# Layer norms' roots as one power on GpSimd, a padded router held while tokens stream, dispatch as steps of its own

## The reference

```python
# attn: 16 heads of 16
h = ln(x); xc = silu(causal_conv4(h))
q, k = l2norm(h@Wq), l2norm(h@Wk); v = ln_per_head(h@Wv)
i = sigmoid(xc@Wig + big); gamma = sigmoid(xc@Wg + bg)
mem_t = gamma_t * mem_{t-1} + (i*k*v)_t
o = groupnorm(ln_per_head(mem) * q) * sigmoid(xc@Wog + bog)
h = x + o@Wo; h2 = ln(h)
out = h + (silu(h2@Wgate) * (h2@Wval)) @ Wout          # hidden width 1024
# moe: 8 experts of 176, top 2 by softmax(x@router.T), weights normalised
routed = sum over the 2 experts of w_e * (silu(x@gate_e) * (x@up_e)) @ down_e
shared = sigmoid(x@shared_gate_w) * (silu(x@sw_gate)*(x@sw_up)) @ sw_down   # width 704
```

## Time and profile before

| | us |
|---|---|
| median of 3 runs | 605.73 |
| lowest, highest | 604.96, 609.38 |
| the profiled execution | 608.32 |
| its span, first to last instruction | 605.9 |
| PE, DVE, ACT, POOL busy | 526.0, 394.4, 261.8, 112.4 |

### The profile page before, as it was taken

How to read it: one execution, slowest core, us unless ns; L and a number is a source line. 1 busy time by engine, 2 the same in 40 slices (tenths; PEclk the granted TensorE clock), 3 DMA queues, 4 the chain that set the end, 5 groups by cost and what they waited for, 6 DMA issues and landing times.

```text
span 605.9 us, 8087 instructions
## 1 busy us (share of the span) xinstructions
PE 526.0 (87%) x2464; PEld 416.9 (69%) x2464; DVE 394.4 (65%) x1159; ACT 261.8 (43%) x465; POOL 112.4 (19%) x133
## 2 busy tenths in 40 slices
PE   2835358999669999999999998999998999999981
PEld 1413234678555687886678786888886799999871
DVE  6786644788774798876488792332649566766437
ACT  4721444625365424365621525311243556666404
POOL 1510003200002323002205000031006024444400
PEclk9985679999769999999999999799998989999997
DMA  8981000000010002111001010010007224444274
GB/s 277 417 235 36 2 2 0 2 10 26 35 35 1 0 19 88 36 35 36 0 2 71 0 36 35 1 41 30 35 8 262 63 64 131 117 140 123 70 273 138
DMA packets 29548, 44.41 MB, mean 73 GB/s; under 512 B 3211, under 2 KB 24203, under 8 KB 29163
## 3 DMA queue, kind: packets, MB, share of 16 engines
q1 hardware_dynamic: 24515, 32.95, 16.9%
q0 software_dynamic: 3408, 9.38, 4.1%
q10 hardware_dynamic: 1584, 1.57, 0.9%
HBM read 27.55 MB, written 16.34 MB: 72 GB/s over the span
## 4 chain that ended last, share of the span: by engine, by line
PE 74%; DVE 16%; ACT 5%; DMA 3%; issue 2%; POOL 0%; ACTq 0%; POOLq 0%; DVEq 0%; SPq 0%
PE psum L768 15%; PE psum L727 12%; PE psum L728 12%; PE psum L729 12%; PE psum L794 5%; PE psum L843 3%; PE psum L737 3%; PE psum L815 3%; DVE XC L1223 2%; PE psum L811 2%; PE psum L829 2%; PE psum L918 1%; PE psum L935 1%; DMA QKV<-x 1%; PE psum L965 1%
## 5 line engine op out<-in xcount | busy, mean ns | idle before, releaser
L637 ACT ACTIVATE SM<-psum 128x512 f32<-128x512 f32 (+1 forms) x56 | 33.3, 596 | 135.0 <-PE psum L729 93.4
L1348 DVE TENSOR_TENSOR SM<-SM,psum 128x512 f32<-128x512 f32 (+1 forms) x56 | 38.3, 683 | 52.4 <-ACT SM L637 48.1
L513 POOL DMA_INDIRECT x_dispatched<-XN,dest x32 | 35.5, 1109 | 163.2 <-DVE XN L1416 154.6
L768 PE MATMUL psum<-WOU,SM 128*128 128x256 f32 x256 | 59.8, 379 | 0.0
L794 PE MATMUL psum<-WQKV,HT 128*128 128x512 f32 (+1 forms) x128 | 51.4, 554 | 6.3 <-ACT QKV L572 2.7
L504 POOL TENSOR_TENSOR OG<-QKV,hvec 128x256 f32<-128x256 f32 x16 | 13.4, 835 | 230.2 <-ACT IG L579 213.4
L768 PEld LDWEIGHTS psum<-WOU,SM 128*128 128x128 f32 x256 | 48.3, 189 | 10.1 <-issue 2.9
L522 POOL DMA_INDIRECT y_routed<-GO,g_dest x39 | 37.7, 967 | 64.1 <-ACT GO L702 63.4
L794 PEld LDWEIGHTS psum<-WQKV,HT 128*128 128x128 f32 x128 | 26.4, 214 | 29.7 <-issue 23.5
L768 PE MATMUL psum<-SDN,SM 128*128 128x256 f32 (+1 forms) x192 | 44.6, 381 | 0.0
L768 PEld LDWEIGHTS psum<-SDN,SM 128*128 128x128 f32 (+1 forms) x192 | 35.8, 189 | 6.6 <-issue 1.3
(11 more groups left out here) (292 smaller groups left out, 1321.2 us busy)
## 6 DMA issues: line engine op xcount, KB each, us to landing
XG<-x_dispatched SPq DMA_DIRECT2D x39, 130.0 KB, 2.7
YF<-y_routed SPq DMA_DIRECT2D x4, 1024.0 KB, 9.1
RUPR<-rup SPq DMA_DIRECT2D x1, 2816.0 KB
X<-x SPq DMA_DIRECT2D x4, 512.0 KB, 6.4
x_after_attention<-X SPq DMA_DIRECT2D x4, 512.0 KB, 2.8
QKV<-x ACTq DMA_DIRECT2D x3, 512.0 KB
y_shared<-SH SPq DMA_DIRECT2D x3, 512.0 KB, 2.9
SHF<-y_shared SPq DMA_DIRECT2D x1, 1536.0 KB
```

What stands on the lines that cost most here:

```text
L513: nc.gpsimd.indirect_dma_start(XD[:, :], bass.IndirectOffsetOnAxis(dest[:, i, old + j:old + j + 1], 0), XN[:, j, :], None).then_inc(dispat ...
L637: nc.scalar.activation(SM[0:rows, g % 3, 0:tb], p_pair(n)[0][0:rows, 0:tb], ACT.Silu).then_inc(silu_ready, 1)
L768: last = nc.tensor.matmul(p_down[:, j // 2, (j % 2) * D:(j % 2 + 1) * D], SM[0:rows, g % 3, j * P:(j + 1) * P], weight[0:rows, m, :], star ...
L1348: nc.vector.tensor_tensor(SM[0:rows, g % 3, 0:tb], SM[0:rows, g % 3, 0:tb], value_rows(n, rows)[:, 0:tb], ALU.mult).then_inc(hid_ready, 1)
```

## The change

**Roots.** The eighteen `rsqrt` calls of layer norms over 256 values (`ln0`, `ln2`, `sum`, `x2`, each once per block, and the two final groups) go. DVE signals `var_ready`, POOL raises variance plus epsilon to the power -0.5 in one `tensor_tensor` with a tile of -0.5 as second operand, signals `root_ready`, and DVE waits for that before the shift. For `ln0` the wait stands at step 2, two steps behind the statistics; for `ln2` and `x2` at step 1, with the shift; for `sum` at step 2; for the final groups at once behind the statistics. The per-head roots stay.

**Router.** Its 9 columns are padded to 128 with zeros and are now the weights of the array; 512 tokens stream: 2 halves x 3 products. The result has the logits on 9 partitions. ACT copies it to LGT, which lies in the memory of SH and so waits for the previous block's store of SH. A new step `logit` turns it back, four PE transposes of 9x128, and DVE copies to LG.

**Choice and dispatch.** `choose` 3 (the weights and tags, DVE) now stands before `rank` (PE and DVE), and the eight indirect DMAs are four steps `send` of two, in blocks 0 to 2 one behind each of the next hidden tiles' down products.

**Memory and loads.** The raw router weights, wg16, wmean and wgx now lie under RUPR and RDNR. So SP waits for `wr_lo` and `wg_ready` before it loads RUPR, and it loads RDNR only behind the last block's stores of `x_after_attention` and `y_shared`, with a wait for the last block's `mup`.

The core of the diff:

```diff
-RP = RW + 1
+RP = P
...
-        late = {0: [("choose", b - 1, 1)], 1: [("choose", b - 1, 2)], 2: [("rank", b - 1, 0), ("choose", b - 1, 3)]} if b > 0 else {}
+        late = {0: [("choose", b - 1, 1)], 1: [("choose", b - 1, 2)], 2: [("choose", b - 1, 3), ("rank", b - 1, 0)],
+                **{m: [("send", b - 1, m - 3)] for m in range(3, 3 + TILES[b - 1])}} if b > 0 else {}
...
-            order += [("xt", b, 0), ("route", b, 0), ("choose", b, 0)]
-    route = {4: [("xt", b, 0)], 5: [("route", b, 0), ("choose", b, 0)], 6: [("choose", b, 1)], 7: [("choose", b, 2)],
-             8: [("rank", b, 0), ("choose", b, 3)]}
+            order += [("xt", b, 0), ("route", b, 0), ("logit", b, 0), ("choose", b, 0)]
+    route = {4: [("xt", b, 0)], 5: [("route", b, 0)], 6: [("logit", b, 0), ("choose", b, 0), ("choose", b, 1)], 7: [("choose", b, 2)],
+             8: [("choose", b, 3), ("rank", b, 0)] + [("send", b, j) for j in range(TILES[b])]}
...
+            wr, wg16, wmean, _, wgx = (first_names.enter_context(nc.sbuf_tensor(k, s, F32)) for k, s in (
+                ("wr", [P, C, RP]), ("wg16", [P, C, HEADS]), ("wmean", [P, C, HEADS]),
+                ("under_rupr", [P, E * C * GU - C * (RP + 2 * HEADS)]), ("wgx", [P, C, D])))
...
+        minus_half = sb("minus_half", [P, 2, max(FIN)])
...
+        LGT = SH[:, :, :].rearrange("p j d -> p (j d)")[0:RW, 0:TB]
...
+            sp.wait_ge(wr_lo, 1)
+            sp.wait_ge(wg_ready, 1)
             sp.dma_start(RUPR[:, :, :, :], rup).then_inc(w_in["routed"], 16)
-            sp.dma_start(RDNR[:, :, :, :], rdn).then_inc(w_in["routed"], 16)
...
             sp.wait_ge(up_psum, done("mup", NB - 1, FM - 1))
+            sp.dma_start(RDNR[:, :, :, :], rdn).then_inc(w_in["routed"], 16)
...
+            def root(kind, n, out, variance, power):
+
+                pool.wait_ge(var_ready[kind], n + 1)
+                nc.gpsimd.tensor_tensor(out, variance, power, ALU.pow).then_inc(root_ready[kind], 1)
+
+            link(nc.gpsimd.memset(minus_half[:, :, :], -0.5))
...
-                if (stage, m) == ("choose", 3):
-                    pool.wait_ge(xn_ready, new)
-                    pool.wait_ge(tag_ready, b + 1)
-                    pool.wait_ge(dest_ready, b + 1)
-                    for j in range(nj):
-                        for i in range(2):
-                            nc.gpsimd.indirect_dma_start(XD[:, :], bass.IndirectOffsetOnAxis(dest[:, i, old + j:old + j + 1], 0),
-                                                         XN[:, j, :], None).then_inc(dispatched, 16)
+                if stage == "send":
+                    if m == 0:
+                        pool.wait_ge(xn_ready, new)
+                        pool.wait_ge(tag_ready, b + 1)
+                        pool.wait_ge(dest_ready, b + 1)
+                    for i in range(2):
+                        nc.gpsimd.indirect_dma_start(XD[:, :], bass.IndirectOffsetOnAxis(dest[:, i, old + m:old + m + 1], 0),
+                                                     XN[:, m, :], None).then_inc(dispatched, 16)
+                if (stage, m) == ("ln0", 1):
+                    root("ln0", b, r01[:, b % 2, :, 0:nj], hva[:, :, 0:nj], minus_half[:, :, 0:nj])
...
+            for g in range(len(FIN)):
+                root("fin", g, fin_r[:, g % 2, 0:FIN[g]], va[:, 0:FIN[g]], minus_half[:, 0, 0:FIN[g]])
...
+                if stage == "route":
+                    act.wait_ge(rt_psum, b + 1)
+                    if b > 0:
+                        act.wait_ge(sh_kept, 16 * b if b < NB - 1 else 16 * (b - 1))
+                    nc.scalar.activation(LGT[:, 0:tb], p_token(b)[0:RW, 0, 0:tb], ACT.Copy).then_inc(rt_kept, 1)
...
+                    for c in range(C):
+                        last = mm3(p_token(b)[:, 0, 0:tb], wrH[:, c, :], wrL[:, c, :], part_h[:, c, 0:tb], part_l[:, c, 0:tb],
+                                   c == 0, c == C - 1)
+                    last.then_inc(rt_psum, 1)
+                if stage == "logit":
+                    pe.wait_ge(rt_kept, b + 1)
                     for j in range(nj):
-                        t = slice(j * P, (j + 1) * P)
-                        for c in range(C):
-                            last = mm3(p_token(b)[:, 0, j * RP:(j + 1) * RP], part_h[:, c, t], part_l[:, c, t], wrH[:, c, :], wrL[:, c, :],
-                                       c == 0, c == C - 1)
-                    last.then_inc(rt_psum, 1)
+                        last = nc.tensor.transpose(p_token(b)[:, 1, j * RW:(j + 1) * RW], LGT[:, j * P:(j + 1) * P], ident[0:RW, 0:RW])
+                    last.then_inc(rt_turned, 1)
...
-                    own = tuple(t[:, :, 0:nj] for t in (hva, hrs, hrt))
                     if m == 0:
                         dve.wait_ge(h_in, 16 * (b + 1))
-                        stats(nj, lambda j: QKV[:, j, 0:D], (hst, hmv, hva[:, 0, :]))
-                        step(nc.vector.tensor_scalar(hva[:, 1, 0:nj], hmv[:, 0:nj, 1], 1.0 + EPS, EPS * EPS, ALU.mult, ALU.add))
-                    if m == 1:
-                        settle()
-                        step(rsqrt(r01[:, b % 2, :, 0:nj], *own))
+                        link(stats(nj, lambda j: QKV[:, j, 0:D], (hst, hmv, hva[:, 0, :])))
+                        nc.vector.tensor_scalar(hva[:, 1, 0:nj], hmv[:, 0:nj, 1], 1.0 + EPS, EPS * EPS, ALU.mult,
+                                                ALU.add).then_inc(var_ready["ln0"], 1)
                     if m == 2:
-                        settle()
+                        dve.wait_ge(root_ready["ln0"], b + 1)
...
-                    link(rsqrt(l2r[:, 0:nj], *scratch(nj)))
+                    dve.wait_ge(root_ready["ln2"], b + 1)
                     minus_mean(nj, l2n, l2r, mv).then_inc(ln2_stats, 1)
...
-                if (stage, m) == ("sum", 1):
-                    step(rsqrt(ers[:, 0:nj], eva[:, 0:nj], ers[:, 0:nj], ert[:, 0:nj]))
+                    stats(nj, lambda j: HR[:, j, :], EXPERTS_OWN).then_inc(var_ready["sum"], 1)
                 if (stage, m) == ("sum", 2):
-                    settle()
+                    dve.wait_ge(root_ready["sum"], b + 1)
...
-                if stage == "route":
-                    dve.wait_ge(rt_psum, b + 1)
-                    nc.vector.tensor_copy(LG[:, 0:nj, :], p_token(b)[:, 0, 0:nj * RP].rearrange("p (j r) -> p j r", r=RP)[:, :, 0:RW]).then_inc(rt_copied, 1)
+                if stage == "logit":
+                    dve.wait_ge(rt_turned, b + 1)
+                    nc.vector.tensor_copy(LG[:, 0:nj, :], p_token(b)[:, 1, 0:nj * RW].rearrange("p (j r) -> p j r", r=RW)).then_inc(rt_copied, 1)
...
+                    dve.wait_ge(picked, b + 1)
...
-                aggregate(nj, (fst, fmv, va))
-                link(rsqrt(r[:, 0:nj], *scratch(nj)))
+                aggregate(nj, (fst, fmv, va)).then_inc(var_ready["fin"], 1)
+                dve.wait_ge(root_ready["fin"], g + 1)
```

More of the change, by code:

```diff
@@ L154, in steps @@
 def steps(engine):
-    attention = [(PLACE[engine][b][i] if b >= 0 else 0, s[0], b + (s in AHEAD), s[1]) for b in range(-1, NB)
+    attention = [(PLACE[engine][b + 1][i], s[0], b + (s in AHEAD), s[1]) for b in range(-1, NB)
                  for i, s in enumerate(ATTENTION) if 0 <= b + (s in AHEAD) < NB]
@@ L234, in build @@
         hst, hmv = sb("hst", [P, J, 6]), sb("hmv", [P, J, 2])
-        hva, hrs, hrt = (sb(k, [P, 2, J]) for k in ("hva", "hrs", "hrt"))
+        hva = sb("hva", [P, 2, J])
         vec = sb("vec", [P, C, NVEC])
         hvec = sb("hvec", [P, 4, HD])
-        wr, wrH, wrL = sb("wr", [P, C, RP]), sb("wrH", [P, C, RP], F32R), sb("wrL", [P, C, RP], F32R)
-        wg16, wgx = sb("wg16", [P, C, HEADS]), sb("wgx", [P, C, D])
-        wmean = sb("wmean", [P, C, HEADS])
+        wrH, wrL = sb("wrH", [P, C, RP], F32R), sb("wrL", [P, C, RP], F32R)
         st, mv = sb("st", [P, J, 6]), sb("mv", [P, J, 2])
         est, emv = sb("est", [P, J, 6]), sb("emv", [P, J, 2])
-        eva, ers, ert = (sb(k, [P, J]) for k in ("eva", "ers", "ert"))
+        eva, ers = (sb(k, [P, J]) for k in ("eva", "ers"))
+        minus_half = sb("minus_half", [P, 2, max(FIN)])
         va, rs, rt = (sb(k, [P, J * 2 * HEADS]) for k in ("va", "rs", "rt"))
@@ L291, in build @@
         ident_zero, ident_ready, halo_zero, same_head = map(sem, ("ident_zero", "ident_ready", "halo_zero", "same_head"))
+        var_ready, root_ready = ({k: sem(f"{k}_{what}") for k in ("ln0", "ln2", "sum", "x2", "fin")} for what in ("var", "root"))
         s_dve, s_act, s_pool = sem("s_dve"), sem("s_act"), sem("s_pool")
@@ L506, in at @@
                     nc.gpsimd.tensor_tensor(vj, vj, per_dim(1, 0), ALU.mult).then_inc(v_scaled, 1)
-                if (stage, m) == ("choose", 3):
-                    pool.wait_ge(xn_ready, new)
-                    pool.wait_ge(tag_ready, b + 1)
-                    pool.wait_ge(dest_ready, b + 1)
-                    for j in range(nj):
-                        for i in range(2):
```

(18 more changed lines are left out.)

8 lines of the change are left out of this document (4 added, 4 removed), and 58 rows, old and new, of the table PLACE.

## The result

The changed kernel takes 604.76 us (median of 13 runs, 602.02 to 607.84) beside 605.73 us of the kernel before (13 runs in turn with them): ratio 0.995, 95% interval 0.9928 to 0.9972. It is half a per cent faster, 3 us by the ratio; I had forecast 13.6. The profiled execution took 606.2 us (span 604.5) against 608.3 (span 605.9).

The account below looks back on a forecast made before the run. PE, busy 526.0 of 605.9 us, was taken as the bound, with DVE or POOL work counting in four places. Terms 7.3 + 1.0 + 1.0 + 1.0 + 1.0 + 0.5 + 1.8 = 13.6 us off 605.7 gave 592, range 586 to 604.

Parts of the forecast that it names:

- roots 4.5: Five exposed roots (block 0's first norm, `ln2` of blocks 0 and 1, both final groups) each 0.9 us shorter on POOL.
- wide router with its clock 5.8: Fewer, wider router products: 1.0 us each in blocks 1, 2 and 3, clock kept 1.0, the rest inside the hand-over.
- order 3.3: New step order: hand-over gain beyond roots and router, plus 0.5 us from weighing ahead of rank in block 3.
- load 0: RDNR loaded behind the last y_shared store, near ACT's use in the last block: cost 0, up to 3 us for the range.
- R: Round trip of a power from DVE over POOL and back: 0.7 us, between 0.3 and 1.8.
- Hand-over, 7.3: Block 0 to block 1, at 150 to 186 us: first hidden product at 178.1 instead of 185.4, 7.3 us saved.
- The opening: Block 0's attention, a serial chain: two exposed roots there save 1.8 us.
- End: Two exposed roots of the final groups: 1.8 us saved.
- third rival: New order gives back its savings (block 1's norm later, or half clock through the hand-over): 599, or 601 with RDNR late; chance 0.22.
- first rival: The power on POOL is slow: gain 9.6 us at R = 1.5, used up at 3.1; chance 0.09.

Follow-up runs that it names:

- the doubled powers: Changed kernel with each power computed twice on GpSimd: 612.68 us, 1.0096 of the kernel before.
- XN first: Changed kernel, RDNR loaded near 340 us, ACT's XN instructions ahead of the HT copies at the hand-over: 600.56 us, 0.9889; second set 600.91, 0.9905.
- the run with the router undone: Changed kernel with the 24 narrow router products back, without the copy and four transposes: 608.76 us, 1.0016 of the kernel before.
- early load: Changed kernel with RDNR's load issued after block 3's last gate product instead of behind its last hidden product: 602.32 us, 0.9929 of the kernel before.
- old order: Changed kernel's roots, router and loads in the kernel before's order of steps: 605.55 us, 0.9967; with RDNR loaded near 340 us 600.68, then 600.86.
- the second trace: Changed kernel run once more without any edit: 604.44 us, 0.9948 of the kernel before.
- both undone: Changed kernel with roots back on DVE and narrow router products, new order and loads kept: 619.63 us, 1.0192 of the kernel before.
- late load in the kernel before: Kernel before with RDNR's load moved from the opening to behind block 3's last hidden product: 611.16 us, 1.0055 of the kernel before.

## Why the prediction was wrong

It was wrong in size: the sign held, the gain was 3 us instead of 13.6. The sum falls into four parts: roots 4.5, wide router with its clock 5.8 (1.8 in the hand-over, four times 1.0), order 3.3 (the rest of the hand-over, and the rank), load 0. All four failed. Timed one by one, roots and router are 1.9 and 3.0 us, the order nothing that can be measured, and the load a loss of 3.3 in the kernel before.

1. **Roots, 4.5: mis-sized.** The count was right, as the doubled powers showed. R, the round trip of a power over POOL, was not: I took 0.7 between bounds of 0.3 and 1.8, and it is 1.12 at 128x4 and 1.74 at 128x8. My reason for the low end was size: a power of few elements is near the iota. But 128x4 to 128x8 adds 0.65 us, 0.16 us per element of a partition, some fifty times the product's 0.0033 (0.84 us for 256). Two narrow roots won 0.5 each, three wide ones lost 0.1 each: 0.7 us by the trace, 1.9 us [0, 3.8] timed. The first power of the run took 1.67 us, like the later ones of its size; the Trainium skill ("GPSIMD Engine Reference", section 2.1) has about 6 us for the first call of a freshly loaded kernel, and no run here shows such a cost.
2. **Hand-over, 7.3, measured 3.0.** The opening missed 1.7 (its two roots gave 0.1), and so OG's product came at 157.71, 1.3 later than my 156.4. `ln2` gave 0.5, not 0.9. Then I took HN to follow its statistics at once, as before. With the shorter DVE chain ACT became the chain: HT held XN up, XN held HN up, 1.2 us; and HN now stands ahead of XTH, so from HN to the router are 3.9 us where there were 2.5. The run with XN first gave 1.0 of this back. That the WO product waits for the HR add and statistics was priced right.
3. **Router, 5.8, measured alone 3.0 us [1.3, 4.5].** Block 1's 2.3 us beside 2.0 is the term that held, but its parts did not: 0.7 are the shorter work (5.2 to 4.5, by the run with the router undone, where 1.0 was forecast), and 1.6 the clock, where I had halved 1.9 for doubt. That the fall stood in the trace of the kernel before was luck: it is in three of six traces with narrow products. Block 2's products ran at half clock behind the same 2.01 us wait: 0.4, not 1.0. Block 3's own share is 0.6 (from its router to the next hidden product 8.89 us instead of 9.48), and a half clock from 447.4 us took it away again in this trace.
4. **Order, 3.3, measured about nothing.** Both new operations with the early load are 0.9879 and 0.9907 in the old order, 0.9889 and 0.9905 in the new one with XN first, 0.9929 [0.989, 0.9968] in the new one as it was. In the changed kernel's trace 1.2 us of what it gave at the hand-over went on ACT's queue there, and 1.0 in TensorE's wait before block 2's router.
5. **RDNR's load, 0, measured 3.3 in the kernel before: the cost that I had described and then put at nothing.** The text has the mechanism, "5 us late, in front of ACT's next silu", with its bound of 3. I took the lower end since RDNR stood behind one store only. It took 13.4 us from issue to use (448.25 to 461.67), more than sup's 10.9, with XF and SHF on its heels, and ACT wanted it at 455.4. In the changed kernel itself the load's cost is smaller and not clear of noise: 1.3 us by the ratios (0.9950 and 0.9929). From the first shared-expert product of the last block to the first waited-for expert product are 33.9 and 33.5 us in its two traces, and 32.4 to 32.5 in four of the five traces of the new order with the early load (33.9 in the fifth).
6. **End.** Of 3.5 us at YF 1.7 went to a half clock in YF's products, which the second trace has not, and 0.2 to the two roots.

Roots and router, 10.3 forecast, are 6.5 us together (0.9879 and 0.9907, old order, early load). With the late load 2.0 of them are left in the old order (0.9967), and 3.0 in the changed kernel. My third rival (0.22; 599 to 601) had the order's term at zero and RDNR 2 us late, but kept R at 0.7. My first rival at R = 1.5 leaves a gain of 9.6; less the order's 3.3 and the load's 3.3 it is 3.0, the time measured. I had held the two apart. That this sum comes out to the tenth is luck: it still has the router at 5.8, where 3.0 was measured, and the roots at 0.5, where 1.9 was.

## What to carry to other kernels

Where an unknown price has bounds of 0.3 and 1.8 us and five exposed steps hang on it, give the sum at both ends, and let two middling mishaps fall in one case of the forecast. Cost a load that moves to just before its use from its issue to its landing, with what follows it on the queue; what it delays is not only the instruction that reads it but all behind that one on the engine. A semaphore that counts two loads makes the reader of the first wait for the second. When one engine's chain gets shorter, read the next engine's queue: here ACT's kept HN 1.2 us, and one changed place in a list gave 1.0 of it back.

## What the runs showed of the hardware

- A power on POOL: 1.01 us at 128x4, 1.65 us at 128x8; products of 128x256 0.84 us.
- Behind the narrow router products of block 1 the granted clock fell to half, TensorE being issued without a pause, in three of six traces with narrow products (1.6 to 1.7 us lost each: before, both undone, late load in the kernel before) and in none of 14 with wide ones. The Trainium skill ("TensorE: Matmul & The Clock Gate", Part 1) ties the clock to how busy PE has been; of the three falls that rule alone doesn't tell.
- A half clock in the last block's hidden tiles costs little where the next stall would have been: there the time lost to the half clock and the time idle trade one for the other (4.9 and 4.0 us in one trace of the changed kernel, 1.7 and 6.4 in the other, from 440 to 490).
- The kernel before has two levels of its own: of its 144 runs 72 took 604.5 to 606.2 us and 65 took 608.6 to 610.4. In the runs of the experiments the lower level goes with a mean granted clock of 0.931 to 0.937, the upper with 0.922 to 0.928. Its profiled run took 608.3 at 0.931. What lowers the clock isn't shown; the levels make any median of it, and each single trace, uncertain by 2 us.
